# Two banks by turns for the up-projections of a tile loop, with a new order of the programs

## The reference

```
x = x + 0.5 * moe0(layernorm(x))        # f = 0: 8 experts, top 2, silu(x Wg) * (x Wu) @ Wd, width 344
x = x + rwkv(layernorm(x))              # f = 1: three projections, a scan over time, one projection
x = x + 0.5 * moe0(layernorm(x))        # f = 2
x = x + 0.5 * moe1(layernorm(x))        # f = 3: 8 experts, top 2, silu(x W1 + b1) @ W2 + b2, width 512
x = x + retention(layernorm(x))         # f = 4: 16 heads of width 8, decayed causal scores, group norm, gate
x = x + 0.5 * moe1(layernorm(x))        # f = 5
```

## Time and profile before

| | us |
|---|---|
| median of 3 runs (lowest, highest) | 915.49 (913.84, 917.21) |
| the profiled execution | 917.44 |
| its span in the trace | 915.6 |
| TensorE busy | 691.8 (76% of the span) |
| GpSimd busy | 432.4 (47%) |
| VectorE busy | 423.0 (46%) |
| ScalarE busy | 362.4 (40%) |
| granted TensorE clock, mean | 0.869 |

### The profile page before, as it was taken

The page is one execution under the profiler, slowest core; times in us unless marked ns, Lnnn a source line. Parts: engine busy times, 40 slices in busy tenths (PEclk is TensorE's granted clock), DMA queues, the critical chain, the costliest instruction groups (busy, mean ns, idle before and its releaser), DMA issues.

```text
span 915.6 us, 15283 instructions
## 1 busy us (share of the span) xinstructions
PE 691.8 (76%) x5116; PEld 590.2 (64%) x5116; DVE 423.0 (46%) x1286; ACT 362.4 (40%) x683; POOL 432.4 (47%) x459
## 2 busy tenths in 40 slices
PE   2488866874687866795878778999739998967683
PEld 2378864674566866684877777656626658866573
DVE  5642235877497613461133213357773576501102
ACT  1244432872386533451332334443424333532231
POOL 2774656553447355535334645621337343354432
PEclk9999897988789887995777988999959999987777
DMA  8812121013102112201211121100211001113202
GB/s 308 324 45 35 41 84 29 19 27 94 36 19 38 41 41 84 61 22 37 72 44 36 42 75 41 25 7 8 87 17 35 11 24 21 44 40 92 44 24 87
DMA packets 42601, 51.77 MB, mean 57 GB/s; under 512 B 7840, under 2 KB 33696, under 8 KB 42400
## 3 DMA queue, kind: packets, MB, share of 16 engines
q0 software_dynamic: 11776, 24.14, 10.7%
q1 hardware_dynamic: 30752, 26.66, 8.9%
HBM read 33.47 MB, written 17.30 MB: 55 GB/s over the span
## 4 chain that ended last, share of the span: by engine, by line
PE 57%; issue 11%; another core or an unknown queue 11%; DVE 10%; ACT 5%; POOL 2%; DMA 2%; SPq 0%; ACTq 0%; DVEq 0%; POOLq 0%
PE bank L545 23%; PE bank L560 13%; PE bank L650 4%; PE bank L547 2%; PE bank L525 2%; PE bank L672 2%; POOL xs L1073 1%; PE bank L628 1%; DVE hT L1288 1%; PE bank L497 1%; ACT hT L841 1%; PE bank L476 1%; ACT w_up L823 1%; DMA xs<-rows_in,take_from 1%
## 5 line engine op out<-in xcount | busy, mean ns | idle before, releaser
L545 PE MATMUL bank<-xT_kept,w_up 128*128 128x128 f32 x1840 | 320.9, 316 | 110.1 <-issue 42.6
L545 PEld LDWEIGHTS bank<-xT_kept,w_up 128*128 128x128 f32 x1840 | 279.0, 215 | 136.5 <-issue 80.9
L1087 POOL DMA_INDIRECT rows_out<-ys,send_to x184 | 187.3, 1018 | 217.4 <-DVE ys L1299 173.5
L1073 POOL DMA_INDIRECT xs<-rows_in,take_from x184 | 181.4, 986 | 170.4 <-PE bank L525 69.9
L560 PE MATMUL bank<-w,hT 128*128 x1288 | 203.8, 304 | 24.1 <-DVE ys L1299 12.2
L560 PEld LDWEIGHTS bank<-w,hT 128*128 128x128 f32 x1288 | 181.0, 215 | 34.2 <-issue 32.6
L823 ACT ACTIVATE w_up<-w 128x728 f32 (+1 forms) x184 | 131.5, 717 | 76.0 <-PE bank L545 29.8
L1299 DVE COPY ys<-bank 128x256 f32<-128x256 f32 x96 | 39.4, 410 | 200.7 <-PE bank L563 104.3
L841 ACT ACTIVATE hT<-bank 128x512 f32<-128x512 f32 x92 | 54.9, 596 | 182.5 <-PE bank L547 103.1
L1288 DVE TENSOR_TENSOR hT<-gate,bank 128x384 f32<-128x384 f32 x92 | 50.7, 551 | 131.3 <-PE bank L545 45.0
L547 PE MATMUL bank<-bconst,bparts 128*128 x368 | 86.1, 234 | 0.0
(11 more groups left out here) (159 smaller groups left out, 748.0 us busy)
## 6 DMA issues: line engine op xcount, KB each, us to landing
yg<-rows_out SPq DMA_DIRECT2D x64, 128.0 KB
w<-in_w SPq DMA_DIRECT2D x8, 536.0 KB, 10.4
rows_in<-xn SPq DMA_DIRECT2D x16, 256.0 KB
w<-in_w SPq DMA_DIRECT2D x8, 512.0 KB
xs<-rows_in,take_from POOLq DMA_INDIRECT x184
rows_out<-ys,send_to POOLq DMA_INDIRECT x184
x<-in_x SPq DMA_DIRECT2D x2, 512.0 KB, 5.6
decay<-in_decay SPq DMA_DIRECT2D x1, 1024.0 KB
```

What stands on the lines that cost most here:

```text
L545: last = mm(to, w_up[:, n % 2, start_col:start_col + P], rows_in, start=True, stop=(k == 0))
L1073: pool.indirect_dma_start(xs[:, q % 2, t, :], None, xn_dram[b], own).then_inc(ld_xs[q % 2][t], 16)
L1087: pool.indirect_dma_start(y_dram[b], own, ys[:, m % 4 // 2, m % 2 * 2 + j % 2, :], None)\
```

## The change

Two things change. The first is the bank. `up_bank` gives the bank of a tile's up-projection: in kind 0 the gate half stays in bank 0, and the up half goes to bank 1 for even tiles and to bank 4 for odd ones. In passes 4 and 7 (`TWO_BANKS`) the tile goes to bank 0 or 1 by turns; in passes 5 and 6, beside which the retention may run, all stays in bank 0. Where two banks are used, the wait is for the reader of two tiles before (`h_done, n - 1`), from the second tile of passes 4 and 7 on. The use of a bank other than 0 is noted in `held`, so that the retention's `take` waits for it, and tiles 0 and 1 of pass 7 wait for the last closing sum where they write bank 1. Readers on ScalarE and VectorE read the bank that `up_bank` names.

```diff
+TWO_BANKS = (4, 7)
...
+        def up_bank(p, j, part=0):
+
+            n = p * TILES + j
+            if KIND[PASSES[p][0]] == 0:
+                return (1, 4)[n % 2] if part else 0
+            return n % 2 if p in TWO_BANKS else 0
...
                 for part in range(2 - k):
-                    if k == 0 and part == 0 and n:
-                        pe.wait_ge(gate_ready, n)
-                    elif n:
+                    own = up_bank(p, j, part)
+                    if k == 0 and part == 0:
+                        if n:
+                            pe.wait_ge(gate_ready, n)
+                    elif k == 0 or j and p in TWO_BANKS:
+                        if n >= 2:
+                            pe.wait_ge(h_done, n - 1)
+                    else:
                         pe.wait_ge(h_done, n)
+                    if p == len(PASSES) - 1 and own and j < 2:
+                        after(RC_DVE, 2 * NB - 1, "x")
+                    if own:
+                        held[own] = h_done, n + 1
                     for c in range(CH[k]):
-                        to = bank[part][:, c * P:(c + 1) * P]
+                        to = bank[own][:, c * P:(c + 1) * P]
...
-                    nc.scalar.activation(hT[:, n % 2, :], bank[0][:], ACT.Silu).then_inc(h_done, 1)
+                    nc.scalar.activation(hT[:, n % 2, :], bank[up_bank(p, j)][:], ACT.Silu).then_inc(h_done, 1)
...
-                V.tensor_tensor(hT[:, n % 2, 0:CH[0] * P], gate[:, n % 2, :], bank[1][:, 0:CH[0] * P], ALU.mult)\
+                V.tensor_tensor(hT[:, n % 2, 0:CH[0] * P], gate[:, n % 2, :], bank[up_bank(p, j, 1)][:, 0:CH[0] * P], ALU.mult)\
```

The second is the order: the tables of TensorE, ScalarE, VectorE and GpSimd are new from end to end, that of SyncE is as it was. A line of it for each of two engines:

```diff
     "pe":
-        "b12 a2 c10 a c a42 c a50 b7 a b4 a3 b a8 b a3 b a10 b2 a14 b2 a b7 a6 b a2 b a8 c2 a c8 a2 c3 a4 c a14 "
+        "b10 c4 b c5 b a2 c a c a45 c a47 b8 a3 b3 a3 b2 a3 b a16 b a5 b a9 b8 a b a6 b a2 b a8 c8 a c3 a2 c2 a3 "
...
     "dve":
-        "b14 c8 b2 c b2 c b7 c9 a2 c a c a2 c2 a17 c a c a17 b3 a b a2 b4 a b2 a b5 a2 b6 a2 b5 a b2 a b2 a b2 a "
+        "b7 c8 b2 c b5 c2 b c b c b2 c b7 c5 a2 c a c a2 c2 a19 c2 a16 b8 a b a2 b a b5 a4 b6 a2 b9 a b2 a b3 a "
```

## The result

The changed kernel takes 947.8 us (median of 4 runs, 940.3 to 954.0) against 914.9 us of the kernel before; the ratio is 1.035 (95% interval 1.027 to 1.043). The forecast was 905, with a range of 888 to 927. Timed again in another group of runs it was 924.0 against 905.3, ratio 1.021 (1.016 to 1.027). The sign holds, the size moves by 1.4 per cent. Ratios are of the runs in each kernel's faster state alone, so the ratio of two medians given beside one can differ from it by up to half a per cent.

The account below looks back on a forecast made before the run. It saw short TensorE waits inside lone expert passes and the hole before pass 6 as the losses. 917.4 - 20 (banks) + 9 (order) = 906.4, forecast as 905 us against the median; own range 897 to 911, 8-in-10 range 888 to 927.

Parts of the forecast that it names:

- The order: New order tables, second retention straight after the first, then all of pass 6 alone: costs 9 us, between -12 and +30.
- first hole: TensorE idle between the last down-projection of pass 5 and the second retention: 6 us and another 4.
- second hole: TensorE idle after the second retention, while pass 6 waits for its route: 16 us, could be 13 or 22.
- TensorE's own work there: Second retention without its tiles: 78.53 less 13 tiles of 2.28, 49 us; VectorE has about as much to do.
- clock terms: Within the order's cost: about 5 us regained from work in the hole at clock 0.65; some 0.4 us lost per pass 6 tile.
- Pass 6 alone: Pass 6 with no retention beside it: takes 75 to 82 us; its 13 moved tiles lose 14 us, 0 to 25.
- over 85: Sign of being wrong: if pass 6 takes over 85 us, the slower rival has it.
- the slower rival: Pass 6 alone runs at 3.7 us a tile, not 3.3, and banks give 6, not 20: 927 us; chance 0.28.
- over 70 us: Sign of being wrong: if the retention alone takes over 70 us, VectorE bounds it and was priced too low.
- The banks: TensorE's waits before up-projections get filled: 6 us in passes 0-3, 11 in 4 and 7, 3 from clock; 20, between 0 and 43.
- the banks' term was an illusion: Sign of being wrong: waits of the down-projections grow by all that the up-projections lose.
- the first rival: Banks give nothing, each late word being met one step later by the down-projection: 913 to 924 us; chance 0.20.

Follow-up runs that it names:

- its late part: All new banks, order of before up to pass 5's fourth tile, new order from there, against the kernel before: 935.5 against 905.3 us, ratio 1.037.
- the early order: All new banks, new order up to pass 5's fourth tile, order of before from there, against the kernel before: 891.2 against 906.2 us, ratio 0.988.

## Why the prediction was wrong, step by step

**The order: +9 was forecast; with the banks of before it cost 42 us (1.046), and its late part alone costs 31 to 40 where the banks are the new ones.** The places were right, one size was not. Against the forecast's list of idle times, the changed kernel's rows above give: first hole 6 + 4, measured 6.1 (15.70 less 9.65; TensorE's last `within` of the first retention waits 5.8 us for a decay product that stands behind the adds on VectorE); inside the second retention 5, measured 14.3; second hole 16, measured 13.5; before pass 7 2, measured 1.8. TensorE's row for the second hole shows the index steps of the route as its longest wait:

```profile
757.00 0.39 PE L516 MATMUL bank<-from_row,in_tile 128*128 128x24 f16 x8 [4.93 <-DVE in_tile L1269]
```

The step that failed is the one that has "TensorE's own work there" as "78.53 less 13 tiles of 2.28", "49 us", taken as the length of the bare retention with 5 and 4 us beside it: 58 us. It took 81.5. I subtracted the tiles from a stage at clock 1.00 and kept the clock; without them the same work is 67.2 us of busy time at 0.81. As an estimate from that row, busy time times clock is 67.16 x 0.81 = 54 us of work at full clock, so 13 of the 18 us of busy time over 49 are the clock and 5 the work. (Of the 13 tiles nine stood beside the retention itself and four beside its closings; they all went behind it.) The page "TensorE: Matmul & The Clock Gate" of the Trainium skill, section "HAM oscillation — how this bites in real kernels", tells of a kernel whose clock falls in waits for DMAs between bursts of matmuls. The rows agree so far as the clock is low in a stretch that waits break up, but the waits here are for VectorE and ScalarE, and from 690 to 700 it is 0.71 with TensorE busy 9.99 of 10 us. The forecast used that section only against the banks. The forecast's clock terms, 5 back from the hole and 5 lost in pass 6, sum to nothing where 25.1 us were lost, and this is most of the 35 us by which the forecast missed between the passes 5 and 7 (9 for 44.4); the retention's idle time is 9 us more.

**Pass 6 alone** was put at 75 to 82 us and took 90.9, 3.95 us a tile. That is past the "over 85" at which the slower rival was to have it. Its reason, the late words that come with indirect DMAs where no retention stands between, fits too: without late words the same 23 tiles took 68.1 us. The rival (927 us, 0.28) had the sign and one of the two places; it had no price on the retention, though the list of what would show me wrong did name "over 70 us". That line gave VectorE as the bound, which is half right: with 11.3 us less of it the stretch was 6.0 shorter.

**The banks: 20 us forecast, 6 measured alone.** Passes 0 to 3 gave nothing (385.8 and 389.8 with two banks, 389.6 with three) where I took 6. In the passes 4 and 7, 11 us of waits were to be filled; 2.8 were, and the rest came back before the down-projection, which the forecast named as the sign that "the banks' term was an illusion". That is the outcome of the first rival, to which I gave 0.20, but its mechanism only in part. Forecast and rival both have the down-projection wait for the silu that the up-projection waited for; that is 8.2 of the 30.0 us, and 21.8 are waits for the copy out of bank 3, which neither names. In the changed kernel against its own order with one bank they did better, 1.021 against 1.046, 23 us across two groups of runs; that order is laid out for them. Without late words they are worth nothing (0.998 and 1.000). The remark of the same section of the Trainium skill that a second PSUM buffer gave no further gain comes nearer to this than my sum; here the time went over to the wait for another bank. (The forecast's figures for that case are 2 us too low: 917.4 + 9 is 926 for the execution and 924.5 against the median, not 924 and 922.)

**The start.** I named only the first norms and put them at nothing. With late words and the third bank the early order as a whole is worth 5 us, not clear of the noise, to 14; in the group without late words it cost 4 us with that bank (756.9 for 752.4) and some 13 without it. I had not looked at it as one thing with the banks. Which of its parts gains, no run shows.

## To carry to other kernels

Before work is taken out of a stage, ask whether the stage gets shorter. If a chain over several engines sets its length, independent work beside it can be free: here 12 tiles cost nothing beside the retention and 4.0 us each behind it. Where it stands matters: ballast at fixed places in the retention's own steps only added to the length. A second buffer fills a wait only if the next step on the same engine is free to go; look at each thing that this step waits for, its own buffer too, before you count the wait as filled. And price every new stage at the clock that its neighbours without filler show, not at that of the stage from which it is cut.

## What was not expected of the hardware

In this kernel the completion words of TensorE come late, by up to several us, and they hang on GpSimd's indirect DMAs: with the 92 of the passes 4 and 7 made plain, of the same bytes, the late words there went from 56 us to 1.4 and both passes lost 52 us together (189.5 to 137.2; one run of each kernel). In the second retention of the changed kernel, where none is issued, no word is late. An indirect DMA took GpSimd 1.0 us and a plain one 0.55, so whether it is the indirection or GpSimd's time on it, these runs don't tell. Nor are they enough for it: from 569 to 653 us in the kernel before GpSimd issues 19 of them without a late word, and in one group of runs the kernel before took 754.6 us for 906, and four kernels near it, with the same 368 indirect DMAs, had none at all. What else it takes, no run shows.
